# Releasing gathered rows and one-hot quarters from VectorE's addition instead of TensorE's sum

## The reference

```
edge_index = jnp.stack([src, dst])
x = _layernorm(x + L0(x, src, dst, edge_weight))      # sum of weighted source rows, then an MLP
x = _layernorm(x + L1(x, W, att, src, dst))           # graph attention, 4 heads of 64
x = _layernorm(x + L2(x, edge_index, ...))            # two attention layers (4 heads, then 1 head of 64), then a projection
x = _layernorm(x + L3(x, edge_index, edge_weight, ...))  # dot-product attention, FFN
```

```
m = segment_max(e, dst);  ex = exp(e - m[dst]);  denom = segment_sum(ex, dst)
out = segment_sum((ex / denom[dst])[:, :, None] * z[src], dst)
```

## Time and profile before

| | us |
|---|---|
| three timed executions | 3131.65, 3132.91, 3138.44 |
| their median | 3132.91 |
| the profiled execution, first to last instruction | 3624.0 |
| granted TensorE clock, mean over that span | 0.719 of full speed |
| busy: PE / PEld / DVE / ACT / POOL | 2348.2 / 1619.2 / 1993.1 / 1393.5 / 2222.1 |

### The profile page before, as it was taken

The page is one execution under the profiler, slowest core; times in us unless marked ns, Lnnn a source line. Parts: engine busy times, 40 slices in busy tenths (PEclk is TensorE's granted clock), DMA queues, the critical chain, the costliest instruction groups (busy, mean ns, idle before and its releaser), DMA issues.

```text
span 3624.0 us, 45558 instructions
## 1 busy us (share of the span) xinstructions
PE 2348.2 (65%) x9551; PEld 1619.2 (45%) x9551; DVE 1993.1 (55%) x7394; ACT 1393.5 (38%) x3670; POOL 2222.1 (61%) x2445
## 2 busy tenths in 40 slices
PE   5555557836677763677776624445455578888888
PEld 2323334724344442344444424444444355656567
DVE  5554446536666674566666723333345356666677
ACT  3444544413333343333333413333343144444444
POOL 5666663566667657666766356666654366666636
PEclk8776667956766687666666755555555799999999
DMA  7655664234444423344444022222212255555511
GB/s 201 177 169 167 174 174 135 63 107 114 116 113 116 115 65 109 105 115 115 114 116 112 21 45 45 47 46 47 47 37 71 69 158 155 153 155 158 149 53 49
DMA packets 247934, 389.14 MB, mean 107 GB/s; under 512 B 58944, under 2 KB 161366, under 8 KB 247673
## 3 DMA queue, kind: packets, MB, share of 16 engines
q0 software_dynamic: 92032, 230.64, 24.4%
q1 hardware_dynamic: 155641, 155.59, 14.0%
HBM read 331.11 MB, written 54.91 MB: 107 GB/s over the span
## 4 chain that ended last, share of the span: by engine, by line
PE 44%; issue 20%; another core or an unknown queue 14%; DVE 13%; POOL 3%; ACT 2%; DVEq 2%; DMA 1%; SPq 0%; POOLq 0%; ACTq 0%
PE PS L1806 22%; PE PS L1727 6%; PE PS L1860 4%; PE PS L1698 4%; DVE ACC L1323 3%; POOL work L690 2%; DVE ACC L1090 1%; DVE work L1294 1%; PE PS L1900 1%; PE PS L1784 1%; PE PS L1843 1%; PE PS L1756 1%; DVEq L376 1%; DMA work<-in_x,srcTile 1%
## 5 line engine op out<-in xcount | busy, mean ns | idle before, releaser
L690 POOL DMA_INDIRECT work<-t_z,srcK x1248 | 1224.4, 981 | 614.1 <-issue 299.6
L1806 PE MATMUL PS<-work,M 128*128 128x260 f32 (+3 forms) x3328 | 1279.3, 505 | 470.8 <-issue 238.9
L1806 PEld LDWEIGHTS PS<-work,M 128*128 128x128 f32 x3328 | 744.2, 266 | 691.1 <-issue 486.0
L1323 DVE TENSOR_TENSOR ACC<-ACC,PS 128x260 f32 (+3 forms) x1614 | 588.1, 364 | 217.8 <-PE PS L1806 122.9
L2034 ACT ACTIVATE M<-iota,dloc 128x128 f32<-128x128 f32 x1248 | 396.9, 389 | 667.5 <-PE PS L1806 360.3
L690 POOL DMA_INDIRECT work<-t_x,srcK x416 | 394.3, 948 | 266.3 <-PE PS L1806 139.7
L690 POOL DMA_INDIRECT work<-in_x,srcTile x392 | 375.8, 959 | 210.6 <-issue 106.9
L1698 PE MATMUL PS<-work,M 128*128 x832 | 310.6, 515 | 252.1 <-issue 138.1
L1698 PEld LDWEIGHTS PS<-work,M 128*128 128x128 f32 x832 | 186.4, 249 | 370.2 <-issue 348.0
L1294 DVE TENSOR_TENSOR work<-work 128x256 f32<-128x256 f32 x800 | 328.7, 411 | 18.5 <-issue 11.7
L1756 PE MATMUL PS<-partsD,work 128*128 x1248 | 235.8, 197 | 143.0 <-DVE junk L1174 96.0
(11 more groups left out here) (267 smaller groups left out, 2918.9 us busy)
## 6 DMA issues: line engine op xcount, KB each, us to landing
work<-t_dhot SPq DMA_DIRECT2D x416, 128.0 KB
t_hot<-M SPq DMA_DIRECT2D x104, 256.0 KB
M<-t_hot SPq DMA_DIRECT2D x104, 256.0 KB
work<-t_z,srcK POOLq DMA_INDIRECT x1248
t_dhot<-work SPq DMA_DIRECT2D x104, 128.0 KB
work<-t_edge SPq DMA_DIRECT2D x104, 64.0 KB
work<-t_x,srcK POOLq DMA_INDIRECT x416
t_z<-Y SPq DMA_DIRECT2D x50, 130.0 KB, 1.9
```

What stands on the lines that cost most here:

```text
L690: pool.indirect_dma_start(out=slots[:, j, 0:width], out_offset=None, in_=table[:, :], in_offset=bass.IndirectOffsetOnAxis(ap=sources[:, k: ...
L1323: ins = vec.tensor_tensor(sums, sums, PS[k % SUMS[stage]][:, 0:cols], ALU.add)
L1806: mm(PS[k % n][:, 0:cols], M[:, k % (4 * G), :], slots_of[:, k % RING[stage], 0:cols], start=True, stop=True)\
```

## The change

Two waits name another semaphore. The values waited for are the same, since both semaphores count one per step and 416 per pass. GpSimd's wait before it overwrites a ring place, and ScalarE's wait before it overwrites a quarter of `M`, are now met by VectorE's addition of that step, not by TensorE's sum of it. L0 keeps its waits. SyncE's wait at line 797 for the loaded one-hots of L3 stays on `step_summed`.

```diff
@@ gather (GpSimd), line 689
                     elif k >= many:
-                        pool.wait_ge(step_summed.sem, step_summed.at(stage, k - many + 1))
+                        pool.wait_ge(sum_added.sem, sum_added.at(stage, k - many + 1))
@@ spread_hots (ScalarE), line 2031
                 if c >= 4:
-                    act.wait_ge(step_summed.sem, step_summed.at(stage, G * (c - 3)))
+                    act.wait_ge(sum_added.sem, sum_added.at(stage, G * (c - 3)))
```

## The result

| | median, us | from, to | timed runs |
|---|---|---|---|
| before | 3135.96 | 3131.65 to 3143.30 | 20 |
| after | 3140.95 | 3137.08 to 3146.94 | 20 |

The ratio is 1.0014, with an interval of 1.0008 to 1.0020: the change costs about 5 us (2.5 to 6.3), a little less than the 0.2% that the prediction called the limit of what can be told. The forecast was 3135.5, +2.6 us on the median then shown (3132.91); 3140.95 lies in its range. Of the 5.4 us between the two, 3.0 are the median of before, which is 3135.96 over 20 runs; the change itself was forecast at 2.6 us and measured at 5.0.

What follows compares the result with a forecast made beforehand. No engine was always busy in the profile; in timed executions GpSimd's issue of gathers was thought the possible bound. 3132.9 + 0 (GpSimd) + 0 (ordinary groups) + 2.6 (last groups) = 3135.5 us, range 3123 to 3154.

Steps and rivals of the forecast that it cites:

- The first rival: GpSimd's ring of gathered rows: the later release starves it and VectorE waits at line 1178; 28 us, 3163 in all, chance 0.16.
- Gathers at 1.25 us bound each pass: Timed executions: GpSimd's issue of 2056 gathers, 2570 us, plus 557 us outside the passes gives 3127, near the median 3132.91.
- GpSimd's later release costs 0: GpSimd's 368 gathers per pass that wait for additions: a lead of 12 to 16 rows covers it, 0 us, at most 112.
- Chunks in ordinary groups: ScalarE's later wait outside the last groups: exponentials still wait for VectorE, margin 1.0 us, cost 0.
- The last two groups of L1 and L2a: ScalarE's chunk 4g+3 delays the scaling TensorE awaits: 3.3 us if all paid, 1.8 for groups 25 alone, 2.6 taken.
- The sum: Whole kernel: 3132.9 + 0 + 0 + 2.6 = 3135.5 us.
- Collision on release: Second rival: released gathers start with VectorE's next operation and last longer; 18 us, 3153 in all, at most 109, chance 0.06.
- The rule of the Trainium skill: GpSimd's DMA descriptors can't be written during VectorE's two-port operations; in full it would add a term of the second rival's size.
- Better phase: Third rival: the new release moves gathers in L1 and L2a away from VectorE's double-input operations; 15 us faster, 3120, chance 0.12.
- Last groups hidden: Fourth rival: VectorE may be further ahead in timed executions, hiding the last groups' cost; 3133, chance 0.66 together with the forecast.
- What would show it: Trace signs: waits move to line 1323, TensorE's four grow to about 13.7 us, line 1178 waits only at pass starts.
- the forecast's second regime: GpSimd itself the bound: the gathers' lead shrinks to nothing, but additions allow 16 rows more than issued, 12 in L3.

## Where the second is met, which the prediction missed

GpSimd at the start of L3, kernel after:

```profile
2506.91 0.95 POOL L690 DMA_INDIRECT work<-t_x,srcK  x1 [0.30 <-issue]
2510.18 0.94 POOL L690 DMA_INDIRECT work<-t_x,srcK  x1 [2.31 <-DVE ACC L1323]
```

The gather at 2510.18 is the 49th of L3, the first that reuses a row. It waits for the addition of step 0, the very first of the pass. Around it, in the same timeline, TensorE and VectorE:

```profile
2507.15 0.60 PE L1806 MATMUL PS<-work,M 128*128 128x257 f32 x2
...
2509.48 0.42 DVE L1323 TENSOR_TENSOR ACC<-ACC,PS 128x257 f32 x1 [0.83 <-PE PS L1806]
```

Step 0 is summed at 2507.75, and the 48th gather ends at 2507.86: by the sum there is no wait at all. The addition ends at 2509.90, and the gather starts 2.01 us later than the usual 0.30 would have it. In e0_before the same gather starts 0.30 us after its forerunner, at 2501.87, while the first addition ends only at 2503.04. The 48 gathers of the ring take 60 us, and in the profiles of the usual kind L3's first addition ends 60.4 to 62.0 us after the pass's first gather. In L1, L2a and L2b it ends 43 to 44 us after it, 17 us before the 49th gather is due, and there no gather behind the first waits over 0.30 us.

The long profile of before had this place too, and all four passes were tight in it. Its 49th gathers in L1, L2a and L2b stood idle for 4.9 to 5.8 us, and that of L3, in the view of the earlier trace rows a part of the 139.7 us, for 52:

```profile
2894.46 0.95 POOL L690 DMA_INDIRECT work<-t_x,srcK  x1 [52.07 <-PE PS L1806]
```

In each of the four the first addition ended 2 to 4 us after the 49th gather had started.

## The experiments

All are against the kernel before, timed in five rounds, and all diffs are against it too. Where an edit adds lines ahead, line numbers in the trace shift by one to four. "Train" is the time from the start of a pass's first gather to the start of its last.

**e0_before.** Nothing edited.

> The kernel before, unchanged, for a profile in which the gathers set the pace as in the timed executions, and for the noise of a comparison. Ratio 1.000 within 0.0007. Theory (gathers bound every pass): the page shows a span near 3134 us, VectorE's line 1178 waits for the gathers' transfers in all 78 groups, some 415 us, and TensorE's four waits for line 2058 sum to about 12 us. For L3 the theory says that GpSimd is held at its 49th gather for less than the 2.3 us that the changed kernel shows there. Rival (the long profile of 3624 us is how the kernel runs): span above 3500 and line 1178 waits only three times.

Measured: 3134.54 us, ratio 0.9995 (0.9986 to 1.0004), span 3130.1. The long profile was an exception, and GpSimd issues all but continuously. Trains of L0, L1, L2a, L2b, L3: 501.7, 540.3, 533.2, 518.7 and 519.8 us. After: 500.0, 543.3, 533.4, 519.0 and 522.7.

**e1_act_only and e2_pool_only.** One half of the change each. In e1 GpSimd's wait is that of before, in e2 ScalarE's.

```
e1 -  act.wait_ge(step_summed.sem, step_summed.at(stage, G * (c - 3)))
e1 +  act.wait_ge(sum_added.sem, sum_added.at(stage, G * (c - 3)))
e2 -  pool.wait_ge(step_summed.sem, step_summed.at(stage, k - many + 1))
e2 +  pool.wait_ge(sum_added.sem, sum_added.at(stage, k - many + 1))
```

> Only ScalarE's wait is changed. Theory (cost sits in the last groups of L1 and L2a, of which those of group 25 are not covered by the gathers): +1.8 us, at most +3.3, ratio 1.0006 (to 1.0011). Rival (all of the 5 us comes from ScalarE, for example through the exponentials in ordinary groups): +5 us, 1.0016. Rival (all comes from GpSimd): 0.

> Only GpSimd's wait is changed. Theory now: GpSimd is held once, at the 49th gather of L3, and this moves L3 by at most 2.3 us: +1.5 to +2.3, ratio 1.0005 to 1.0007; in L1, L2a and L2b no gather has an idle time over 0.31 us. Forecast as made: 0. Rival (ring starved): +3 to +5 us with line 1178's waits longer inside the passes.

Measured: e1 3137.18 us, ratio 1.0004 (0.9993 to 1.0015); e2 3134.00 us, 0.9993 (0.9984 to 1.0002). Neither is told apart from no change. The interval of e1 (-2.2 to +4.7 us) holds what its half would cost by the trace; that of e2 (-5.0 to +0.6) ends just below the 0.8 us that its hold would cost, in rounds in which the unchanged kernel itself came out at -1.6. The traces do tell the halves apart: in e1 VectorE's waits for line 2224, at the ends of L2a and L2b, are 7.1 us for 6.1 in e0_before, the growth all in L2a, and chunk 4g+3 waits for line 1323; in e2 the only hold of GpSimd is the 49th gather of L3, 1.09 us idle. TensorE's four waits in e1 are 12.6 us (2.52, 3.86, 2.52, 3.70). This sum is no measure of the cost by itself: a first wait of a pass is over 1 us shorter in some profiles, as the 1.89 in L1 of e8_l3_start_late8 for the 3.15 of e0_before, though both kernels have the waits of before there.

**e3_act_last and e4_pool_l3_start.** Only the two places at which the costs are met.

```
e3 +  gate = sum_added if stage in ("L1", "L2a") and c >= CHUNKS - 8 and c % 4 == 3 else step_summed
e4 +  gate = sum_added if stage == "L3" and k < 64 else step_summed
```

> ScalarE's wait is changed only for the second chunk after the weights (4g+3) in groups 24 and 25 of L1 and L2a, four waits in all. Theory: the same as with all of ScalarE's waits changed, +1.8 us (to +3.3), and TensorE's four waits for line 2058 are 2 to 3.6 us longer in sum than in the kernel before. Rival (ordinary groups carry the cost): 0.

> Only gathers 48 to 63 of L3 wait for the addition, all else waits as before. Theory (the one place where GpSimd is held is the 49th gather of L3): that gather is held 1 to 2.3 us, L3's train of gathers from first to last lasts 1 to 2.9 us longer than the 519.8 us of the kernel before, and the other passes keep their length. Whole time +1 to +2.3 us, ratio 1.0003 to 1.0007, too little for the interval alone. Rival (the hold is regained later in the pass): L3's train within 0.5 us of 519.8.

Measured: e3 3135.76 us, 1.0000 (0.9991 to 1.0009); e4 3136.52 us, 1.0007 (0.9998 to 1.0016). TensorE's waits in e3 are 14.8 us (3.51, 3.86, 3.69, 3.71), so nearly the whole growth of the waits is made by these four chunks; e4 has the hold, 1.07 us idle, and a train of L3 of 520.9. As times, costs of 1 to 3 us are below what five rounds resolve. So I went over to enlarging each suspect.

**e5_pool_late8.** GpSimd waits for an addition eight steps later still, in the passes L1, L2a and L2b.

```
+  pool.wait_ge(sum_added.sem, sum_added.at(stage, k - many + (9 if stage in GAT else 1)))
```

> GpSimd waits in L1, L2a and L2b for an addition eight steps later than it needs, and in L3 for the addition as in the changed kernel. Theory (16 rows of headroom while the gathers set the pace): no gather of L1, L2a and L2b is held, the trains of gathers stay at 541, 534 and 519 us within the 3 us by which L1's differs between profiles, ratio 1.000 to 1.001. Rival (the ring is starved by a later release): holds in every group, at least 1 us in each of 78 groups, ratio 1.02 or more.

Measured: 3134.44 us, 0.9998 (0.9989 to 1.0007). Even so no gather of these passes waits for an addition over 0.30 us. GpSimd's waits in L1 of e5:

```profile
POOL work L690 <- issue: 92.6, 304, 0.3
POOL work L690 <- DVE ACC L1323: 33.2, 109, 0.3
```

The first rival, a ring that starves, is refuted for these passes: there are at least eight more steps in hand than the change uses. In L3, where its wait is that of the changed kernel, the 49th gather stands idle for 2.31 us and the train is 522.6.

**e8_l3_start_late8.** The hold at L3's start enlarged: for k < 64 of L3 the addition eight steps later.

```
+  gate = sum_added if stage == "L3" and k < 64 else step_summed
+  pool.wait_ge(gate.sem, gate.at(stage, k - many + (9 if stage == "L3" and k < 64 else 1)))
```

> Gathers 48 to 63 of L3 wait for an addition eight steps later than they need; all else waits as before. Theory (a hold at the start of L3 is never regained, since from then on the gathers set the pace): the hold of 1.1 us grows by eight steps of VectorE, 8 to 12 us, L3's train of gathers grows from 519.8 to about 530 us, and the whole by as much, ratio 1.003. Rival (the ring's lead pays it back): train and time within 3 us of before.

Measured: 3143.20 us, 1.0019 (1.0009 to 1.0028), +6 us (2.8 to 8.8). GpSimd in e8:

```profile
2505.95 0.94 POOL L691 DMA_INDIRECT work<-t_x,srcK  x1 [8.64 <-DVE ACC L1324]
2507.58 0.94 POOL L691 DMA_INDIRECT work<-t_x,srcK  x1 [0.68 <-DVE ACC L1324]
2508.99 0.95 POOL L691 DMA_INDIRECT work<-t_x,srcK  x1 [0.47 <-DVE ACC L1324]
```

The held gathers lose 8.34 + 0.38 + 0.17 = 8.9 us over the usual 0.30, and the train of L3 is 529.0 us for 519.8, 9.2 more. Nothing is won back in the 365 gathers that follow. In time, 6 us arrive (at most 8.8), somewhat less than the 8.9 of this one profile; how long the hold was in the other executions isn't known. By this the 2.0 us of the kernel after are lost too: its train of L3 is 522.7, and e5's, with the same hold, 522.6, where the profiles without a hold have 519.4 to 521.3. The 1.0 of e11 (520.7) is too small to be seen among those.

**e6_act_late3.** ScalarE's wait three steps later still in all but the last two groups, to eat the margin ahead of the exponentials.

```
+  late = 0 if c >= CHUNKS - 8 else 3
+  act.wait_ge(sum_added.sem, sum_added.at(stage, G * (c - 3) + late))
```

> ScalarE waits for an addition three steps later than it needs, in all groups but the last two of each pass, where its wait is that of the changed kernel. Each step is about 0.7 us of VectorE's work, so chunk 4g+1 ends after VectorE has released the exponentials, by about 1 us, and these start late. Theory (VectorE then waits 5 us for the gathers in each group, so that a late exponential is covered): only the cost of the last groups remains, +2 to +3 us, ratio 1.001, and line 1178's waits shrink from 415 us by up to 78. Rival (late exponentials reach the end): +50 to +80 us, ratio 1.016 to 1.025.

Measured: 3139.31 us, 1.0014 (1.0005 to 1.0023). The exponentials are late now, which is seen from the two sides of line 2021:

```profile
DVE junk L1178 <- DMA work<-t_z,srcK: 328.9, 73, 15.7
...
PE PS L1789 <- ACT work L2021: 154.7, 78, 2.4
...
ACT work L2021 <- DVE work L1279: 115.0, 35, 26.6
```

TensorE's waits for line 2021 are 154.7 us for 29.9 in e0_before, but VectorE's waits for rows shrink by 66 us (328.9 for 395.1): much of the delay is taken out of time in which VectorE would wait for gathers. What reaches the end is +4.4 us (1.6 to 7.2), which holds the last groups' cost, as this kernel has it as well, and excludes the +50 of the rival. The profile can't say more: its span of 3129.2 us is no longer than that of e0_before, since its gathers of L1 were faster (a train of 534.7 for 540.3). So late exponentials are covered by the gathers, and in the kernel after they aren't late in the first place.

**e7_scale_first.** In groups 24 and 25 of L1 and L2a the scaling stands ahead of chunk 4g+3, with the waits of before.

```
-  spread_hots(stage, 4 * g + 3)
-  for k in range(GS * g, GS * (g + 1)): ... the scaling
+  if not helped:
+      spread_hots(stage, 4 * g + 3)
+  for k in helped: ... the scaling
+  if helped:
+      spread_hots(stage, 4 * g + 3)
```

> Waits as before, but in groups 24 and 25 of L1 and L2a ScalarE scales its rows ahead of chunk 4g+3, not behind it. Theory (the wait for line 2058 is on the path in group 25 of both passes, and covered by the gathers in group 24): TensorE's four waits of 2.9 us shrink to about 1 us each, and the time falls by 2 x 1.9 = 3.8 us, ratio 0.9988, or less if VectorE or GpSimd is next. Rival (the scaling isn't on the path): 0.

Measured: 3134.76 us, 0.9997 (0.9987 to 1.0007): no gain where I had expected 3.8 us. Waits in e7, and TensorE in L1, group 25, which has its weights at 1184.37:

```profile
PE PS L1806 <- ACT work L2058: 4.4, 4, 1.3
...
DVE nodeC L1393 <- ACT nodeB L2226: 6.1, 4, 3.9
```

```profile
1187.42 1.58 PE L1806 MATMUL PS<-work,M 128*128 128x260 f32 x6 [1.08 <-ACT work L2058]
...
1191.63 0.79 PE L1806 MATMUL PS<-work,M 128*128 128x260 f32 x2 [1.32 <-DVE work L1294]
```

The waits for the scaling fall from 11.7 to 4.4 us, and TensorE goes on 3.05 us behind the weights, not 4.88 as in e0_before. But six MATMULs later it waits for a row that VectorE scales. From the weights of L1's group 25 to the first gather of L2a are 55.25 us in e7 and 55.24 in e0_before. So an earlier scaling wins nothing, because VectorE's rows hold TensorE next, and the rival is right for a gain. It doesn't follow that a later scaling costs nothing.

**e9_chunk_ahead.** The waits of before; in groups 24 and 25 of L1 and L2a chunk 4g+2 moves ahead of the exponentials and weights, so that less is left behind them.

```
+  ahead = helper(stage, GS * g + 1) == "scalar"
+  if ahead:
+      spread_hots(stage, 4 * g + 2)
   ... the weights
-  spread_hots(stage, 4 * g + 2)
+  if not ahead:
+      spread_hots(stage, 4 * g + 2)
```

> Waits as before, but in groups 24 and 25 of L1 and L2a ScalarE makes chunk 4g+2 before the exponentials, in the 2.0 us in which it waits for VectorE, not behind the weights. Theory (at the end of L1 and L2a ScalarE's total work behind the weights, two chunks and the scaled rows, is what the end waits for): one chunk of 1.9 us less behind the weights, with exponentials up to 0.5 us later, so each of the two passes ends 1 to 1.9 us earlier: -2 to -3.8 us, ratio 0.9991. Rival (the end waits for something else): 0.

Measured: 3133.32 us, ratio 0.9982 (0.9973 to 0.9991): 5.6 us faster than before (2.8 to 8.5), the lowest ratio here; the medians are 3.5 us apart (3133.32 and 3136.79). TensorE's waits for the scaling fall from 11.7 to 8.7 us, and VectorE's at the ends of L2a and L2b from 6.1 to 5.3:

```profile
PE PS L1806 <- ACT work L2062: 8.7, 4, 2.5
...
DVE nodeC L1393 <- ACT nodeB L2228: 5.3, 4, 3.0
```

The time fell at least as far as the theory said, but the trace doesn't show its mechanism. The stretch from L1's last gather to L2a's first is 70.45 us and the next one 74.35 (70.08 and 73.86 in e0_before), where the theory has each 1 to 1.9 us shorter. In L1, 0.35 us are won behind the weights of group 25, but these come 0.7 us later. The profile's span is 3131.9, and its train of L2a (531.7 us) is the shortest of all. Why e9 is faster stays open.

**e10_act_longer.** Sixteen small ScalarE instructions that write an unread tile, ahead of chunk 4g+3 in the same four groups. They take 3.06 us together.

```
+  if stage in ("L1", "L2a") and c >= CHUNKS - 8 and c % 4 == 3:
+      turn = (2 if stage == "L2a" else 0) + (1 if c == CHUNKS - 1 else 0)
+      for i in range(4 * G):
+          sc.activation(spare[:, turn, i, :], iota[:, 0:1], ACT.Abs, ...)
```

> Waits as before, but sixteen small ScalarE instructions stand ahead of chunk 4g+3 in groups 24 and 25 of L1 and L2a, about 3 us in each; they write a tile that nothing reads. Theory (group 24 is covered by the gathers, group 25 is not): the stretch from the last gather of L1 to the first of L2a, and the one from L2a to L2b, grow by about 3 us each, +6 us, ratio 1.002. Rival (all four are paid, as the forecast had it for the slow profile): +12 us, 1.004. Rival (none is on the path): 0.

Measured: 3147.55 us, 1.0036 (1.0024 to 1.0049), +11.3 us. L1, group 25 in e10:

```profile
1191.52 3.06 ACT L2037 ACTIVATE spare<-iota,dloc 128x1 bf16<-128x1 f32 x16
...
1196.31 3.91 ACT L2063 ACTIVATE work<-work 128x64 f32<-128x64 f32 x16
...
1197.41 2.97 PE L1807 MATMUL PS<-work,M 128*128 128x260 f32 x6 [5.88 <-ACT work L2063]
```

Four delays of 3.06 us are 12.2, of which 11.3 arrive (7.5 to 15.4): more than group 25's alone (6.1), as I had taken for the gather-bound case. The trace says the same: the two stretches between the passes are 75.8 and 80.4 us, 5.7 and 6.6 more than in e0_before, where I had expected 3 each. The exponentials of group 25 start 17.3 and 16.4 us after the pass's last gather (14.2 and 14.3 in e0_before), so 2 to 3 us of group 24's delay reach group 25. From the weights of L1's group 25 to the first gather of L2a are 57.8 us for 55.2, so of that group's 3.0 us about 2.5 are paid. A delay of 3 us is paid almost in full in all four groups; for one of 0.9 us this doesn't follow, as the table below shows.

**e11_after.** The changed kernel once more, in the rounds of the others.

> The changed kernel once more, beside the others on one chip. Theory: +4 to +5 us, ratio 1.0014, within 1.0008 to 1.0020; the stretch from L1's last gather to L2a's first 1 us longer than before, the next 1 to 2 us longer, and L3's 49th gather held 1.1 to 2.3 us.

Measured: 3139.69 us, 1.0010 (1.0001 to 1.0019). The four waits are 15.1 us again, and L3's 49th gather stands idle for 1.27 us (2.31 in the first profile), with a train of L3 of 520.7. The two stretches between the passes, expected 1 and 1 to 2 us longer, are 70.5 and 73.7, 0.4 more and 0.2 less than in e0_before: this expectation failed. One profile is too few for it, as all of them together show (us from the start of a pass's last gather to the start of the next pass's first):

| runs | L1 to L2a | L2a to L2b |
|---|---|---|
| ScalarE's waits of before (e0, e2, e4, e5, e8) | 70.1 to 70.5, mean 70.3 | 72.2 to 74.8, mean 73.8 |
| ScalarE's later wait in the last groups (after, e1, e3, e6, e11) | 70.5 to 71.5, mean 71.1 | 73.7 to 76.6, mean 75.5 |
| e7, e9 | 70.4, 70.5 | 74.7, 74.4 |
| e10 | 75.8 | 80.4 |

The later wait costs 0.8 us at the end of L1 and 1.7 at the end of L2a, 2.5 together, with the second uncertain by its spread. TensorE's waits are 3.4 us longer, so part of that is covered. In L1 it can be seen where: from the weights of group 25 to the first gather of L2a are 55.2 to 55.4 us in the five profiles of the first row and 55.7 to 55.9 in those of the second, 0.5 us for a chunk that is 0.95 later.

## Why the prediction was right, and where it was not

1. *Gathers at 1.25 us bound each pass in the timed executions.* Right in kind, and the step that helped most, as it was read out of a profile of an execution that was bound otherwise. The 78 waits of VectorE for rows and the closely packed gathers of GpSimd show it. That the sum of 3127 came so near was in part luck: in e0_before the five trains take 2614 us, not 2570 (1.30 us for each gather in L1 and 1.28 in L2a), and all else 516, not 557. The two errors nearly cancel.
2. *GpSimd's later release costs 0, since 12 to 16 rows are in hand.* Right for L1, L2a and L2b: shown by e5, with eight steps to spare. Wrong at the start of L3, and this is the step that failed. The lead was read in the middle of L1 and by the slots of a running pass; the fill of the ring was not looked at. There the 49th gather waits for the first step of all, and the first addition of L3 comes 61 us after the first gather, that of L1 43 us; why L3's is so late was not tested. It cost 2.0 us in one profile and 1.0 in another; that such a hold isn't won back in the pass is shown by e8. The trace of before had the place (the 52.07 above), and in its long execution the later release would have held all four passes there.
3. *Chunks in ordinary groups: 0, margin 1.0 us.* Right: the exponentials still wait for line 1279 in all 104 groups. In L1's group 25 of the kernel after the fade stands at 1186.76 and ends 1187.01, and the exponentials start at 1188.04 when VectorE lets them: 1.0 us. (Step 4c is 13 steps after the one that chunk c waits for, not 12, which changes nothing.) What I hadn't said is that beyond the margin the gathers cover it too. "Each 0.1 us more costs 0.1 in each of 78 groups" is wrong in a usual execution (e6).
4. *The last two groups of L1 and L2a: 0.90, 0.90, 0.90 and 0.61 us.* The mechanism is right, and the sum of 3.3 us is met by TensorE's waits (15.1 less 11.7 is 3.4). Of this 2.5 us reach the next passes by the table above, so the 2.6 that the forecast took is met, in part by luck. Its reason is only half right: the gathers don't hide all that group 24 loses (e10), and group 25, taken as paid in full, has 0.5 us covered in L1.
5. *The sum.* 2.5 here and 1.0 to 2.0 at the start of L3 are 3.5 to 4.5 us; 5.0 is measured, 2.5 to 6.3 by the interval, and 3.1 in e11 (0.3 to 6.0). That the two account for all of it is an inference from sizes: no run has taken both away and left the rest of the change in, each half alone was too small to be told in time, and a shift of 1 us in the trains of L1 would not be seen among their spread.
6. *Rivals.* A starved ring: refuted (e5). Collision on release: where GpSimd's gathers are let go by an addition, they keep their means within 8 ns, so no term of its kind shows. (The counts behind its bound, 68, 50 and 80 waits, are 71, 38 and 88 in the trace, and 52 us of L3's sum are a single wait.) That gathers last 1005 ns in L1 and 946 in L2b is so in both kernels. The rule of the Trainium skill ("SBUF — State Buffer", "SBUF: two separate sides") speaks of VectorE's two-port modes, and no run here shows whether VectorE was in one, so it is neither borne out nor refuted. In L1 of e0_before VectorE's row scaling (line 1294) runs during 52% of the time of the 105 gathers that last over 1.0 us, and during 25% of that of the others, so the two may well be connected; no experiment took it away. Better phase: the gathers of L1 do take 409.3 us in e6 and 415.9 in the kernel after, and L1's train 534.7 and 543.3, so a phase worth several us exists. The change can't be seen in it: L1's train is 539.0 to 543.1 us in the profiles with ScalarE's old wait (e0, e2, e4, e5, e8) and 540.4 to 543.3 in those with the new one at the last groups (after, e11, e1, e3). L2a's train leaves room for a phase that costs: it is 531.7 to 533.9 us in seven of the eight profiles with the old wait (536.1 in e10), 533.4 and 532.8 in the kernel after and e6, but 536.1, 536.0 and 537.2 in e1, e3 and e11. No experiment tested this, so a cost of up to 3 us by phase in L2a stays an open rival. Last groups hidden: refuted by e10 for a delay of 3 us; for the change's own delay the table speaks against it, through means of few profiles.
7. *What would show it.* The signs for the moved waits and for TensorE's four (10.4 to 13.7 foretold, 11.7 to 15.1 found) held. Those drawn from the one long profile failed, in both kernels alike: line 1178 waits in every group, not only at pass starts, and line 1199 waits for transfers inside L3 (54.6 us, 57.5 in e0_before), which was to mean that the forecast is wrong; and the lead of the gathers is nothing, not 12, as the forecast's second regime has it. None of these comes from the change. Sums less additions are 200 to 199, for the three of the earlier trace rows, by these windows of the kernel after (L690, L1806, L1323, 305 us from the start of L1):

```profile
627.00:932.00 305.00, 231.62 (x232) 0.66 0.47 128
...
627.00:932.00 305.00, 180.82 (x400) 87.90 (x401) 0.66 0.47 128
...
627.00:932.00 305.00, 81.35 (x199) 0.66 0.47 128
```

The additions allow 199 + 48 = 247 gathers, and 232 are out. GpSimd is 15 behind what it may do, where the long profile had it one behind the earlier trace rows.

## What to carry to other kernels

In this kernel, a wait that was moved to a later event of the same step cost nothing where the passes ran steadily. Look for its cost at the fill (the first reuse waits for the first step of all) and at the end (what stands behind it is awaited and no transfer covers it). Before any sum, hold the span of the profile against the timed median: here they were 16% apart, and the count of the gathers times their spacing said what the timed executions were bound by. When a suspected cost is smaller than the timing resolves, enlarge it at its place and read the trace and the time together; but a delay of 3 us that is paid almost in full doesn't say that one of 0.9 is (0.5 us of it were covered here), nor that the same place gains by being sooner (e7 gained nothing). And compare the same group in both traces: here two groups of a pass look alike and differ by 0.3 us in what the change does to them.

## What the runs showed of the hardware that I had not expected

- GpSimd issues an indirect gather of 128 rows each 1.25 us, very evenly in L2b, where VectorE's row operations are narrow: 518.7 to 519.2 us for the 415 spacings in all thirteen profiles of after and the experiments. In L1 the same 415 spacings differ by up to 9 us from profile to profile (534.7 in e6, 543.5 in e10); what sets it in a given execution stays open.
- One profiled execution of the same kernel was 494 us longer than the next (3624.0 to 3130.1), with L1's train at 602.4 us for 540.3. It wasn't seen again in thirteen more profiles, and its cause stays open.
